# Macaron layer stack on one Trainium2 core: block weights loaded from the SyncE queue, the first expert bias and the score masks added by TensorE, hidden high and low parts taken straight from PSUM, paired banks with wide calls

## The reference

```
x = x + 0.5 * moe(layernorm(x))      # 8 experts, top 2, D_FF = 512
x = x + attention(layernorm(x))      # 16 heads of 8, rotary, causal
x = x + 0.5 * moe(layernorm(x))      # the same experts again
x = x + 0.5 * mx(layernorm(x))       # linear 128x128 on values rounded to a 6-bit grid by blocks of 32
x = x + gated(layernorm(x))          # scan over tokens, then a gated feed-forward of 384
x = x + 0.5 * mx(layernorm(x))

moe:        out += (relu(z @ W1[e] + b1[e]) @ W2[e] + b2[e]) * gate[e]   for the two chosen experts e
attention:  softmax(where(causal, Q @ K.T / sqrt(8), -inf)) @ V, heads joined, times W_o
```

## Time and profile before

| | us |
|---|---|
| median of 3 runs | 1554.93 (1553.53 to 1559.62) |
| time of the profiled execution | 1563.51 |
| its span | 1561.5 |

### The profile page before, as it was taken

The page is one execution under the profiler, slowest core; times in us unless marked ns, Lnnn a source line. Parts: engine busy times, 40 slices in busy tenths (PEclk is TensorE's granted clock), DMA queues, the critical chain, the costliest instruction groups (busy, mean ns, idle before and its releaser), DMA issues.

```text
span 1561.5 us, 22422 instructions
## 1 busy us (share of the span) xinstructions
PE 1110.2 (71%) x7265; PEld 802.5 (51%) x7265; DVE 950.8 (61%) x2549; ACT 711.8 (46%) x1651; POOL 837.5 (54%) x1081
## 2 busy tenths in 40 slices
PE   1066666899957798987788888878995458574263
PEld 1066654655656665655555564545564446552232
DVE  4354554657644755665658574846557867867746
ACT  2154532456734445663354465535553355453141
POOL 1448655556565674662657553467345683545312
PEclk9999877899976879997888888979996679787576
DMA  9867656644456754445354464244323433410000
GB/s 312 294 212 259 199 199 190 210 136 139 147 181 210 237 185 159 132 153 169 123 187 154 140 184 128 66 158 147 114 84 113 131 129 119 165 49 22 14 1 14
DMA packets 88931, 232.82 MB, mean 149 GB/s; under 512 B 15216, under 2 KB 47344, under 8 KB 72432
## 3 DMA queue, kind: packets, MB, share of 16 engines
q0 software_dynamic: 25472, 142.94, 27.8%
q1 hardware_dynamic: 63344, 88.45, 17.8%
HBM read 175.48 MB, written 55.33 MB: 148 GB/s over the span
## 4 chain that ended last, share of the span: by engine, by line
PE 44%; DMA 12%; DVE 12%; POOL 12%; issue 10%; ACT 6%; SPq 4%; POOLq 0%; DVEq 0%; ACTq 0%
PE bank L531 39%; PE bank L543 5%; DMA Qs<-q_scratch 4%; POOL z_scratch L1420 3%; DMA q_scratch<-ab 3%; DVE hlo L971 2%; POOL yg L1452 2%; POOL wt L1434 2%; POOL hhi L1442 2%; DMA P<-in_w 2%; ACT hfull L1262 2%; DMA k_scratch<-ab 1%; SPq L489 1%; SPq L501 1%; DVE sm_m L1031 1%
## 5 line engine op out<-in xcount | busy, mean ns | idle before, releaser
L531 PE MATMUL bank<-hhi,wt 128*128 128x256 f32 x960 | 232.1, 336 | 105.3 <-DVE hlo L971 102.3
L1031 DVE TENSOR_REDUCE sm_m<-bank 128x4 f32<-128x512 f32 x320 | 212.4, 683 | 139.6 <-PE bank L531 139.4
L971 DVE TENSOR_TENSOR hlo<-hfull,hhi 128x512 fp32r<-128x512 f32 x240 | 194.8, 825 | 134.5 <-POOL hhi L1442 134.3
L531 PE MATMUL bank<-zh,wt 128*128 128x256 f32 x1440 | 244.8, 319 | 17.1 <-DVE zh L963 11.2
L1262 ACT ACTIVATE hfull<-bank,wt 128x256 f32<-128x256 f32 x480 | 198.4, 477 | 106.8 <-PE bank L531 103.7
L531 PEld LDWEIGHTS bank<-hhi,wt 128*128 128x128 f32 x960 | 173.1, 222 | 137.0 <-DVE hlo L971 119.7
L531 PEld LDWEIGHTS bank<-zh,wt 128*128 128x128 f32 x1440 | 214.1, 219 | 34.9 <-issue 12.8
L1434 POOL DMA_INDIRECT wt<-w_scratch,ei x120 | 123.8, 1031 | 197.5 <-ACT yb L1270 175.3
L1313 ACT ACTIVATE P<-bank 128x512 f32<-128x512 f32 x320 | 180.8, 601 | 96.4 <-PE bank L531 95.5
L1442 POOL TENSOR_SCALAR hhi<-hfull 128x512 fp32r<-128x512 f32 x240 | 163.0, 687 | 99.4 <-ACT hfull L1262 96.1
L1420 POOL DMA_INDIRECT z_scratch<-zb,pos x128 | 135.5, 1058 | 86.0 <-DVE pos L952 51.6
(11 more groups left out here) (183 smaller groups left out, 1879.5 us busy)
## 6 DMA issues: line engine op xcount, KB each, us to landing
zin<-z_scratch SPq DMA_DIRECT2D x120, 128.0 KB
y_scratch<-yt SPq DMA_DIRECT2D x120, 128.0 KB, 2.7
w_scratch<-wt SPq DMA_DIRECT2D x8, 1024.0 KB, 13.3
q_scratch<-ab SPq DMA_DIRECT2D x32, 256.0 KB, 4.2
k_scratch<-ab SPq DMA_DIRECT2D x32, 256.0 KB, 3.4
Ks<-k_scratch SPq DMA_DIRECT2D x64, 128.0 KB, 3.7
Qs<-q_scratch SPq DMA_DIRECT2D x64, 128.0 KB, 3.9
P<-in_w SPq DMA_DIRECT2D x8, 512.0 KB, 11.3
```

Of the source, the lines that this page charges most:

```text
L531: return e.matmul(o, lhs, rhs, start=start, stop=stop, **kw)
L971: e.tensor_tensor(hlo[s % 4][:, :, :], hfull[s % 3][:, :, :], hhi[s % 4][:, :, :].bitcast(F32), ALU.subtract).then_inc(*d_hid.step(s, "lo"))
L1031: e.tensor_reduce(bn_m[:, k, s_, :], blocks(shared("maxi", i, 0, s_)), AX.X, ALU.max).then_inc(*d_max.step(i, f"m{s_}"))
```

## The change

- `wload` moves from POOL to SP. DVE's routing now leaves the plain expert number in `ei`; SP reads it into a register (`value_load`) and issues two plain DMAs: the 1 MB of weights, and 4 KB with the high and low part of `b1`, two rows, into `wb`.
- In `hid`, each of the two chunks begins with a matmul of these two rows against a tile of ones (2 partitions deep, `tile_position` 0, 32, 64 or 96); the six others follow.
- ACT's `hid` step is one call over 512 columns with relu, writing `hhi` rounded; POOL's step is gone, and so is `hfull`; DVE computes max(PSUM, 0) minus `hhi` in one call. The bank is held until DVE is done.
- `res` starts when `hhi` is there: four matmuls with `hhi`, then a wait for `hlo`, then the two with `hlo`.
- In `scor`, PE adds the mask of the diagonal blocks by bf16 matmuls after each score matmul pair, as `maxi` does; POOL's `affine_select` is gone.
- The six banks become three aligned pairs; `maxi` and `scor` take a whole pair, and DVE's maximum and ACT's exponential are one call over 1024 columns.
- The table of durations and predecessors is changed to match, so all streams are in another order.

```diff
-    "wload": ("G1.1+6", [], 1),
+    "wload": ("S.3+6", [], 1),
-    "hid": ("P.72 A.85 G.68 D.8", [(0, 1)], 1),
+    "hid": ("P.95 A.6 D.7", [(0, 2)], 1),
-    "maxi": ("P.5 D.69 D.69", [(0, 1, 2)], 1),
+    "maxi": ("P.5 D1.22", [(0, 1)], 1),
-    "scor": ("P.45 A.6 A.6 G.46<1 G.46<2", [(0, 1, 2)], 1),
+    "scor": ("P.6 A1.03", [(0, 1)], 1),
...
+            def wload(u):
+                f, k = divmod(u, KB)
+                w.wait_ge(*d_route.at(f, "ei"))
...
+                if u >= WR:
+                    w.wait_ge(*t_res.at(2 * (u - WR) + 1, "y"))
+                    w.wait_ge(*a_yout.at(u - WR, "y"))
+                row = e.value_load(ei[0:1, f % 2, k:k + 1], min_val=0, max_val=NE - 1)
+                e.dma_start(wt[u % WR][:, :].bitcast(F32), wd[bass.DynSlice(row * 128, 128), :]).then_inc(l_wt[u % WR], 16)
+                at = 32 * (u % WR)
+                e.dma_start(wb[at:at + 2, :].bitcast(F32), bd[bass.DynSlice(row * 2, 2), :]).then_inc(l_wt[u % WR], 16)
...
             def hid(s):
                 u = s // 2
-                o = take("hid", s, 0, a_hid.at(s, "h")).rearrange("p (c t) -> p c t", c=2)
+                o = take("hid", s, 0, d_hid.at(s, "lo")).rearrange("p (c t) -> p c t", c=2)
...
-                    mm(o[:, c, :], w1[:, 0, cs], z[:, 0, :], c == 0, False, skip_group_check=True)
+                    mm(o[:, c, :], wb[at:at + 2, cs], oner[at:at + 2, :], c == 0, False, skip_group_check=True,
+                       tile_position=(at, 0))
+                    mm(o[:, c, :], w1[:, 0, cs], z[:, 0, :], False, False, skip_group_check=True)
...
             def res(s):
-                w.wait_ge(*d_hid.at(s, "lo"))
+                w.wait_ge(*a_hid.at(s, "hi"))
...
+                w.wait_ge(*d_hid.at(s, "lo"))
+                for c, cs in enumerate(cols):
                     t = mm(o, w2[:, 0, cs], hlo[s % 4][:, c, :], False, s % 2 == 1 and c == 1)
...
             def scor(i):
...
+                def diags(*cols):
+                    for s_ in range(2):
+                        for col in cols:
+                            t = mm(shared("scor", i, 0, s_)[:, col:col + 128], mask[:, :], identb[:, :], False, True,
+                                   skip_group_check=True)
                     return t
...
                 elif k < 4:
                     scores(k - 2, 3, 384, True)
-                    t = scores(k - 2, 1, 0, True)
+                    diags(384)
+                    scores(k - 2, 1, 0, True)
+                    t = diags(0)
...
# DVE
-                e.tensor_tensor(hlo[s % 4][:, :, :], hfull[s % 3][:, :, :], hhi[s % 4][:, :, :].bitcast(F32), ALU.subtract
-                                ).then_inc(*d_hid.step(s, "lo"))
+                e.scalar_tensor_tensor(out=hlo[s % 4][:, :, :].rearrange("p c t -> p (c t)"), in0=shared("hid", s, 0), scalar=0.0,
+                                       in1=hhi[s % 4][:, :, :].rearrange("p c t -> p (c t)").bitcast(F32), op0=ALU.max,
+                                       op1=ALU.subtract).then_inc(*d_hid.step(s, "lo"))
# ACT
-                for c in range(2):
-                    k = 2 * (s % 2) + c
-                    t = e.activation(hfull[s % 3][:, c, :], o[:, c, :], ACT.Relu, bias=b1[:, k:k + 1])
-                t.then_inc(*a_hid.step(s, "h"))
+                e.activation(hhi[s % 4][:, :, :].rearrange("p c t -> p (c t)"), shared("hid", s, 0), ACT.Relu
+                             ).then_inc(*a_hid.step(s, "hi"))
...
-                for s_ in range(2):
-                    e.activation(P[:, (2 * i + s_) % PR, :], shared("scor", i, 0, s_), ACT.Exp, scale=SCALE
-                                 ).then_inc(*a_sc.step(i, f"e{s_}"))
-                    yield
+                at = 2 * i % PR
+                e.activation(P[:, at:at + 2, :].rearrange("p s q -> p (s q)"), wide("scor", i, 0), ACT.Exp, scale=SCALE
+                             ).then_inc(*a_sc.step(i, "e"))
# POOL
-            def hid(s):
-                w.wait_ge(*a_hid.at(s, "h"))
...
-                e.tensor_scalar(hhi[s % 4][:, :, :], hfull[s % 3][:, :, :], 1.0, 0.0, ALU.mult, ALU.add).then_inc(*p_hid.step(s, "hi"))
```

178 lines of the change are left out of this document (88 added, 90 removed).

## The result

The changed kernel takes **1717.5 us** (median of its runs, 1697.9 to 1741.9) beside 1557.3 for the kernel before on the same chip. The ratio, **1.095** with a 95% interval of 1.086 to 1.103, is of the fast runs alone (1697.9, 1700.5 and 1714.9 us, mean 1704); the medians by themselves would give 1.103. The forecast was 1582 us, 1.7% slower, with a range up to 1650. The direction was right, the size was not: the time lies outside the range, and what happened is rival B, to which I had given 0.08. Where the executions of the changed kernel differ, the granted clock differs with them: 0.80 in the 1734.6 us of the profiled one, 0.82 in the shortest two.

What follows compares the result with a forecast made beforehand. PE was taken to lead in the middle, step latency to count as much outside it. 1563.5 + 126 (PE work) - 84 (off the chain) - 15 (clock) = 1590.5, less 8.6 gives 1582 us; range 1495 to 1650.

Steps and rivals of the forecast that it cites:

- rival B: Much slower: PE becomes the bound in the middle stretch, keeping its fill of 84%; 1681 us, chance 0.08.
- What bounds the kernel: No engine full; PE leads from 240 to 1140 us at 84% busy, outside it step latency counts as much.
- price of 0.62: Share of PE's busy time on the chain, charged per added us: 204 us of PE work gives +126 us.
- Bias matmuls: Two added per hid step on PE, 0.30 us each, 0.60 a step: 144 us over 240 steps, range 58 to 192.
- Score masks: Mask matmuls on PE in scor: 1.9 us a group, 60 us over 32 groups, low end 41.
- What leaves the chain: POOL's rounding 31 us, DVE's hlo 23, ACT's single call 9, wload's issue 21: together -84 us.
- The other half: PE's wait for DVE's hlo falls below 30 us, and PE waits for ACT's hhi instead.
- Edits at nothing: POOL's relief, wide calls over 1024 columns, banks held longer and taken in pairs: 0 us, 15 kept for the range.
- SP: Register load and two issues for wload, 1.2 us in a block of 13 us on average: hidden.
- The clock: More PE work in the middle raises the granted clock from 0.85 by some hundredths: -15 us.
- A: Faster: PE's whole 102 us wait for hlo goes, 1503 us; or lone shallow matmuls pace like the rest, 1529; chance 0.33.
- C: Slower: 1 MB weight loads stand ahead of small ones in SP's queue, 1629 us, chance 0.09.

Runs made afterwards that it cites:

- the kernel with selectors: Changed kernel with all experts' biases in one 128-row tile, full-array bias matmuls, no bias loads, score masks on POOL: 1454.5 us, 0.934 on a chip N, 0.983 on chips S.
- chips S: Chips where profiles of kernels descended from the changed one show PE and ACT standing still without recorded reason; the changed kernel took 1813.7 us, 1.155 of before.
- chip N: A chip where those profiles show no such standing stretches; the changed kernel took 1717.5 us, 1.095 of before.

## Why the prediction was wrong

**What bounds the kernel.** Right as a reading: PE leads in the middle, latencies outside. I wrote that the price of 0.62 "would rise if PE became fuller", and then used 0.62 for 204 us of added work on a PE that was 84% full. That is the first of the two steps that failed. For the masks 0.62 was right: 37 and 41 us paid on 60. For the bias the runs show 214 to 232 us paid on 242, 0.88 to 0.96; and where only the form is changed 190 to 208 on 187 (240 x (1.72 - 0.94)) and 104 to 121 on 91. The last two look like more than one for one because 187 and 91 are taken at full clock; by the mean steps they are 197 and 101 to 130, about one for one.

**Bias matmuls.** The second step, and the mechanism in it was right: the term was mis-sized. I took 0.30 each and 0.40 as the upper end: 0.09 going in and 0.31 to the next. Measured are 0.505, 242 us in all where I had 144. The missing tenth is behind it: the three full matmuls that follow take 0.55 instead of 0.35, so both changes are paid in full, in and out. I had argued the change out down to 0.21, because the row with 0.31 had a pair ahead of it. Even 0.80 a step, my end, falls short of 1.01. What I had taken, 0.60, is what the two cost when they stand side by side (1.34 - 0.71 = 0.63).

Neither step alone breaks the range. With 242 for 144 and the price kept, the sum is 1582 + 98 x 0.62 = 1643; with 144 kept at a price of 0.96 it is 1582 + 144 x 0.34 = 1631. With what the bias really cost, 214 to 232 in place of 144 x 0.62 = 89, it is 1707 to 1725, and 1717.5 was measured, 1704 by the three runs of the ratio. That this comes so close is partly luck, as the next terms were off too.

**Score masks.** Right: a unit of 1.12 us, and 37 and 41 us in the time on two chips. In the kernel with selectors the masks on PE cost more, 66 us.

**What leaves the chain.** 84 us was too much on chips S: 18 to 25. On a chip N the kernel with selectors is 103 us faster than the kernel before with 480 more full matmuls in it, so there the rest of the change, without the small bias load, seems worth at least that; no run on a chip N takes it alone. The wait itself went as said, PE's for `hlo` from 102 to 20 us, and so did the calls: ACT's at 596 ns where I said 0.60, DVE's at 687 where I said 684.

```profile
L1028 DVE SCALAR_TENSOR_TENSOR hlo<-pair,hhi 128x512 fp32r<-128x512 f32 x240 | 163.9, 687 | 281.0 <-ACT hhi L1314 280.7
L1314 ACT ACTIVATE hhi<-pair 128x512 fp32r<-128x512 f32 x240 | 143.1, 596 | 392.4 <-PE pair L569 392.3
```

The other half, that PE should wait for ACT's `hhi` instead, didn't come: by its groups PE waits 3.0 us ahead of the `hhi` matmuls, for `yb`.

**Edits at nothing.** Wide calls: nothing measurable, in one kernel. The paired banks, also at nothing, were not undone alone, so that is not shown. SP: the register load shows as

```profile
L511 SPq TENSOR_LOAD <-ei x120: 432/442/1099, 63.1 to 1547.4; - x120
```

0.44 us, and SP has 1% of the chain. The small bias load, which I had in SP's 1.2 us and nowhere else, shows some 15 us where it is the only difference, not clear of noise. The Trainium skill, page "DMA: Bandwidth & Descriptors", section "Latency and other measured facts", has a floor of about 600 ns for the register load; the measured 442 ns are below it, and the measurement decides.

**The clock.** Wrong in sign: -15 us forecast. The stretch in the middle lost 0.04 to 0.07. I had read from before that slices with a fuller PE have the higher clock. The kernels now say it is not PE's busy share: 95 and 96% busy with lone shallow matmuls give 0.78 and 0.81, 94% with paired ones 0.85, 83% with full ones 0.87, and 91% without masks but with lone ones on a chip S 0.76:

```profile
240.00:1140.00 900.00, 815.47 (x4503) 532.73 (x4502) 424.81 (x1093) 335.55 (x598) 171.41 (x171) 0.76 0.42 135
```

Masks are full-array work, and taking them out didn't raise the clock. The lower clock goes with the lone matmuls; of two kernels on one chip that differ in their grouping and in the order, the one with half the changes of form has 0.85 and the other 0.81. I can't say from these rows whether the array's fill or its standing still between forms is what counts.

**The rivals.** B named what happened, with the right place and a wrong price: it reckoned with 145 x 0.60 where 145 x 1.01 is true, and with a steady clock, and came to 1681. With 0.505 in its place, (145 x 1.01 + 60) / 0.84 + 95 x 1.01 x 0.62 - 84 - 8.6 + 1563.5 = 1776, too much, as PE's fill rose to 95% instead of staying at 84%; with 0.95 in the first term it is 1748, and 1717 was measured. B deserved more than 0.08: it needed only that the lone matmul cost the sum of its two rows, 0.40, which gives 1728 by the same sum. A was wrong: the waits that it counted on did go, but they were refilled by PE's own work. C is not seen: DMA fell from 12% to 4% of the chain.

## What to carry over

Ahead of adding a small matmul to a stream of full ones, ask which form it has. Rows of zeros cost nothing that shows here (0.11 us for the selector's matmul of 128 rows), a change of form does: 0.39 us at full clock for each matmul that stands alone in another form, more than three full matmuls. If it must be another form, put such matmuls side by side. When a term is taken from a row that shows a pair, the lone case belongs at or above its upper end and not below. And try the price of one for one beside the share of the chain when the engine is over 80% full and the added work fills it: the bias was paid at 0.88 to 0.96, the smaller mask term at 0.62 to 0.68. Reckon such work at both levels of the clock, not at the full one alone.

When kernels of different batches disagree with one theory after another, put the anchors (the kernel before, the changed one, one variant) on one chip before a third theory is made. Not doing so cost me two wrong readings here.

## What I hadn't expected of the hardware

- One matmul moved by three places in each step gives 104 to 121 us, and the clock in the middle goes from 0.81 to 0.85.
- The four row positions of the 2-partition matmul cost the same, position 0 included.
- A moving operand that repeats one column 256 times paces as any other, 0.11 us.
- The same kernel differs by 5.6% (1717 and 1814 us) and by 6.2% (1454 and 1544) between chips, while the kernel before differs by 0.9%. A ratio from one chip is not a property of a kernel alone.
